# Two drains on GpSimd in a two-layer gated kernel: one between the expert layers, one in every pair of the second

## The reference, cut to what matters

```python
x = x + jnp.tanh(g_xattn[0]) * _L0_xattn_ref(_layernorm(x), ctx_1024, ctx_1024)      # decayed running sum over the batch axis
x = x + jnp.tanh(g_ffn[0]) * _L0_ffn_ref(_layernorm(x), Wg, W_in, W_out)             # expert layer 0: 8 experts, top 2, capacity
x = x + jnp.tanh(g_xattn[1]) * _L1_xattn_ref(_layernorm(x), ctx_1024, ctx_1024, ...) # masked causal attention
x = x + jnp.tanh(g_ffn[1]) * _L1_ffn_ref(_layernorm(x), gate_w, w1, w2)              # expert layer 1: 8 experts, top 2
```

```python
logits = jnp.einsum('td,ed->te', xt, gate_w)
w_topk, sel = jax.lax.top_k(logits, K)            # K = 2
w_topk = jax.nn.softmax(w_topk, axis=-1)
combine = zeros((T, E)).at[arange(T)[:, None], sel].add(w_topk)
h = jax.nn.silu(jnp.einsum('td,edf->tef', xt, w1))  # 256 -> 1024 features
y = jnp.einsum('tef,efd->ted', h, w2)               # 1024 -> 256
out = jnp.einsum('ted,te->td', y, combine)
```

## Time and profile before

| | |
|---|---|
| median of the runs | 586.25 us |
| the profiled execution's own time | 586.66 us |
| its span, first to last instruction in the trace | 584.5 us |
| mean granted TensorE clock | 0.945 |
| PE busy | 523.4 us, 90% of the span |
| POOL busy | 250.9 us, 43% |

### The profile page before, as it was taken

How to read it: one execution, slowest core, us unless ns; L and a number is a source line. 1 busy time by engine, 2 the same in 40 slices (tenths; PEclk the granted TensorE clock), 3 DMA queues, 4 the chain that set the end, 5 groups by cost and what they waited for, 6 DMA issues and landing times.

```text
span 584.5 us, 12291 instructions
## 1 busy us (share of the span) xinstructions
PE 523.4 (90%) x3955; PEld 497.3 (85%) x3960; DVE 338.3 (58%) x800; ACT 323.5 (55%) x667; POOL 250.9 (43%) x281
## 2 busy tenths in 40 slices
PE   2889879999999999998992389999999999999990
PEld 1678779999999999986872289999999999999990
DVE  1888844855665575384778855465536463644531
ACT  3565425756666674524676446565646564655640
POOL 2400475664446451331000254456654665455452
PEclk9996799999999999989997579999999999999996
DMA  7952353345354433451122534645644464443322
GB/s 257 367 192 90 105 186 103 127 149 167 94 169 149 170 99 105 164 176 61 34 84 75 115 120 111 187 108 117 144 99 108 111 124 116 92 133 46 47 38 41
DMA packets 52453, 72.74 MB, mean 124 GB/s; under 512 B 7200, under 2 KB 43936, under 8 KB 52416
## 3 DMA queue, kind: packets, MB, share of 16 engines
q1 hardware_dynamic: 40752, 50.34, 26.2%
q0 software_dynamic: 11664, 21.94, 17.8%
HBM read 51.54 MB, written 20.73 MB: 124 GB/s over the span
## 4 chain that ended last, share of the span: by engine, by line
PE 79%; DVE 10%; issue 3%; DMA 3%; ACT 2%; POOL 1%; DVEq 0%; SPq 0%; ACTq 0%; POOLq 0%
PE PA L1678 27%; PE PC L1678 18%; PE PD L1678 18%; PE PB L1508 3%; PE PD L1508 2%; PE PB L1690 2%; PE PB L1864 2%; DMA xg<-xn_rows,row_x 1%; PE PB L1502 1%; PE PC L1508 1%; DVE stats L982 1%; DMA cx<-ctx 1%; PE PA L1542 1%; DVE ys L1122 1%; DVE xs L1291 1%
## 5 line engine op out<-in xcount | busy, mean ns | idle before, releaser
L1678 PE MATMUL PA<-xhi,whi 128*128 128x256 f32 (+1 forms) x440 | 129.3, 294 | 5.1 <-issue 3.5
L1678 PE MATMUL PA<-xlo,whi 128*128 128x256 f32 (+1 forms) x440 | 126.3, 287 | 0.0
L1678 PE MATMUL PA<-xhi,wlo 128*128 128x256 f32 (+1 forms) x440 | 126.3, 287 | 0.0
L1242 DVE TENSOR_TENSOR hlo<-cT_all,hhi 128x512 fp32r<-128x512 f32 x78 | 54.0, 694 | 111.3 <-ACT hhi L929 111.2
L927 ACT ACTIVATE cT_all<-PA 128x512 f32<-128x512 f32 x78 | 46.6, 597 | 91.5 <-PE PA L1678 83.8
L597 POOL DMA_INDIRECT out<-ys,row_o x38 | 62.9, 1656 | 75.8 <-DVE ys L1449 70.0
L1678 PEld LDWEIGHTS PA<-xhi,whi 128*128 128x128 f32 x440 | 84.8, 193 | 6.5 <-issue 4.8
L1678 PEld LDWEIGHTS PA<-xlo,whi 128*128 128x128 f32 x440 | 84.8, 193 | 0.0
L1678 PEld LDWEIGHTS PA<-xhi,wlo 128*128 128x128 f32 x440 | 84.7, 193 | 0.0
L1678 PE MATMUL PD<-whi,hhi 128*128 128x256 f32 x284 | 81.1, 285 | 0.4 <-DVE wlo L1193 0.4
L1678 PE MATMUL PD<-wlo,hhi 128*128 128x256 f32 x284 | 80.3, 283 | 0.0
(11 more groups left out here) (265 smaller groups left out, 1182.0 us busy)
## 6 DMA issues: line engine op xcount, KB each, us to landing
raw<-w SPq DMA_DIRECT2D x16, 1024.0 KB, 5.7
raw<-L_ffn_W_in SPq DMA_DIRECT2D x8, 1024.0 KB
raw<-L_ffn_W_out SPq DMA_DIRECT2D x8, 512.0 KB
y_rows<-ys SPq DMA_DIRECT2D x8, 512.0 KB, 7.8
xn_rows<-xn SPq DMA_DIRECT2D x8, 512.0 KB, 3.4
xs<-x SPq DMA_DIRECT2D x4, 512.0 KB, 7.0
cx<-ctx SPq DMA_DIRECT2D x4, 512.0 KB, 7.7
ys<-y_rows SPq DMA_DIRECT2D x4, 512.0 KB, 4.3
```

The source lines that it names most:

```text
L1242: return dve.tensor_tensor(dst, src, hi.bitcast(F32), ALU.subtract)
L1678: mm = pe.matmul(dst, a[k], b[k], start=(first and k == 0 and a is lhs_hi and b is rhs_hi), stop=(last and k == n - 1 and a is lhs_lo))
```

## The change

Two lines are added. `pool.drain()` stands once behind the loop of `share`, ahead of the subtraction that waits for `oh_ready`; and once at the end of `free1`, behind the wait for the scatter-adds and behind the increment of `ys1_free`. `free1` is written out for each pair, so the program has 24 drains more, and 20 of them run where there are 19 pairs: 1 between the layers, 15 inside the loop over the first 16 pairs, 1 behind that loop, and 3 in the pairs behind it. No drain has a wait or an increment of its own. No other instruction is added, taken away or moved.

```diff
@@ -558,6 +558,7 @@
             pool.wait_ge(gates_ready, 1)
             for q in range(1, NQ):
                 share(q)
+            pool.drain()
 
             gate_step = (NQ - 1) * K + 1
             pool.wait_ge(oh_ready, 2)
```

## The result

The kernel became faster. Twelve runs of the change had a median of 580.81 us (576.62 to 582.65), twelve runs of the kernel before 583.79 us (582.45 to 588.26). The ratio is 0.9922, with a 95% interval of 0.99 to 0.9945. The runs before lie in two groups, near 583 and near 587 us, so their median says less than their mean: the means are 580.35 and 584.76 us, 4.41 us apart, and agree with the ratio. The forecast was no change, 586.4 us.

A forecast was written before the change was run, and what follows sets the result against it. The prediction took PE to bound the kernel, with the end waiting for POOL's last scatter-add and the program's close. Its terms, 0 + 0 + 0 + 0.15 us on the median of 586.25 us, gave 586.4 us, range 583.0 to 589.0.

The forecast's parts named there:

- What bounds the kernel: Whole kernel: PE, busy 90% of the span, sets the time; a POOL delay costs nothing until PE runs out of work.
- The last drain: Behind the last scatter-add's landing, where the program closes: nothing covers the added drain, so it costs + 0.15 us.
- What one drain takes: Price x of one GpSimd drain, bounded from other instructions' rows: 0.15 us, with ends at 0.05 and 0.32 us.
- Between the layers: Drain behind the last addition of share: covered by 43.62 us of POOL idle time before the subtraction, cost 0.
- Fifteen drains in the loop: First sixteen pairs, ahead of the scatter-adds: some 3.30 us of free POOL idle time covers each drain, cost 0.
- releaser no longer evac1: Sign against the forecast, in the loop: a pair's first scatter-add is started by something other than VectorE's evac1.
- The 0.57 us of overlap: In each pair, a gate operation overlaps the scatter-add before it; the drain lies ahead of the scatter-adds, so term 0.
- Drain behind the loop and three pairs: Ahead of the last three pairs' gates: slack of 0.29, 1.24 and 1.24 us takes in one x each, cost 0.
- the first scatter-adds start as long after evac1 as before: Expected sign in the last pairs: idle times of 0.59, 1.54 and 1.54 us shrink by x, starts against evac1 unchanged.
- The dear drain: Last pairs: a costly GpSimd drain exceeds the slack, adding 4x - 2.77 us from x = 0.92 us; chance 10%.
- The moved code: POOL's code behind 24 more instructions: shifted fetching stalls in the last pairs, up to a few us, 587 to 589; chance 4%.
- Cheaper scatter-adds: GpSimd's scatter-adds: drains order the work and make later ones cheaper, 585.3 us at a third off; over 1% faster, chance 2%.

## Why the prediction was wrong

**What bounds the kernel:** right. PE bounds the pairs, and POOL is off the path until its last scatter-add. The gain lies wholly outside that bound.

**The last drain: the step that failed.** I wrote that behind the last landing "the program closes and the span ends at 584.5 us", added x for the new drain, and left the rest as it stood. Those 6 us were nearly four fifths one instruction of GpSimd, 4.68 us, and its length depends on what the change does. The term was + 0.15 us and measured + 0.37 for the new drain and - 4.63 for the old one. Every other step asked who waits for whom; this one took a stretch of 1.4% of the span as fixed because no engine had a row in it. I cited the Trainium skill, VectorE: DVE Perf Modes, section The DRAIN you can't avoid, for 12 ns for the drains that the runtime places around a kernel, and then wrote that no row of the trace shows one. Line L106 shows five. They carry a line of the kernel, so whether they are the drains that the section means isn't shown; what they take is measured: 7 and 8 ns on SyncE and ScalarE, 73 on TensorE, 179 on VectorE and 4682 on GpSimd, and here the measurement decides.

**What one drain takes:** wrong by more than a factor of ten in the loop, and by 2.5 in the last drain, the one that counted. x = 0.15 us, with ends at 0.05 and 0.32, came from other engines' sequencers. On GpSimd it is 0.04 to 0.05 us with nothing owed (the lower end), 0.37 us in the last pairs, and up to 8.77 us in the loop. And the sentence that bounded it from below, that a gain is no part of the price "since nothing is removed", was the one that closed off the answer: a drain shortens the next one.

**Between the layers:** right at 0. The 7.8 us are twice my far bound of 3.9 us and a fifth of the idle time.

**Fifteen drains in the loop:** right at 0, for a partly wrong reason. I had 3.30 us of slack before the scatter-adds and the gathers' landing at 367.0 us. The landing takes up to 7.6 us, and the drain, not evac1, set the start of the scatter-add in 14 of 15 pairs. What held was the cover behind it, the buffers of ys that VectorE needs two pairs later. So the sign "releaser no longer evac1", which I gave as one that would make the forecast wrong, came up and cost nothing. The 0.57 us of overlap that I weighed lies outside the drain.

**Drain behind the loop and three pairs:** right at 0. The last pair's gates came 0.3 us later against evac1, its second gather ended 1.08 us ahead of evac1 as before, and PE's stretch is the same, 213.83 us. The sign that the first scatter-adds start as long after evac1 as before failed by 0.19 us, to the good.

**The sum:** 0 + 0 + 0 + 0.15 us was + 0.37 - 4.63 us, with 0.30 us more at the branches. That 94% went to "within 1%" and the gain was 0.8% is luck: the closing drain stood in no term and no rival.

**The rivals.** The dear drain was right that a drain is dear, and its formula has the place right too: the kernel with drains only from the loop's last pair on is that rival, and slower. In the change it doesn't happen, because the drains ahead of it have paid: four DMAs' worth is left, 0.37 us. The moved code is out as a cause of the gain; it cost 0.30 us. Cheaper scatter-adds are out: 63.6 us for 38 of them, against 62.9. The mechanism that happened was none of mine.

## What to carry to other kernels

Read the rows of the stretch behind the last compute row, the closing line of each sequencer too, before you call it fixed: something there may depend on the whole program. If GpSimd issued DMAs, look at its closing drain; a drain of your own where GpSimd has slack and the queue behind it is not urgent takes that time off the end. Pay often or early enough that no drain owes much, and last near the end: one that paid for the whole program in the last pairs cost PE 7.56 us.

## What the runs showed of the hardware

A drain on GpSimd waits for the operation that is running (1.99 us against an addition of 1.90) and for the landing of the DMAs that GpSimd has issued (it ends 0.20 us after the last increment in 14 of the change's 15 drains in the loop). Behind DMAs that have all landed it takes 82 ns for each since the last drain, measured at 2, 4, 6, 14, 30, 46, 62 and 70 of them, the first of the 70 some 200 us before. With none, it takes 41 to 50 ns. So the landing of a DMA, and a wait for it by semaphore, leave something undone on GpSimd that a drain finishes.

Two things stay open. What is done for each DMA was not measured, only its time. And with more DMAs the drain can be shorter than the rule: 82 cost 3.70 us and 167 cost 4.68 us at the close, 155 cost 7.34 us behind the loop, while the 85 ahead of the drain between the layers cost about 7.0 us, which the rule gives. Some of a long debt is cleared without a drain; when, these runs don't tell.
